# fp16 parts for the queries, keys and states of the last two attention blocks, and other orders in pairs 10 to 12

## What is computed

```python
x = x + attn(layernorm(x))
x = x + ffn(layernorm(x))

# attention, for each sequence and head; k is scaled to norm 1
attn    = (q @ k.T) * beta.T * decay                # within a chunk
y_local = attn @ v
delta   = v.T @ (k * beta * decay_to_end)
y       = (q @ state.T) * exp(cla) + y_local         # chunks in turn
state   = state * total_decay + delta

# ffn: Wg, Wu, Wd are 4-bit codes times scales
gate, up = xt @ Wg.T, xt @ Wu.T
out      = (gelu(gate) * up) @ Wd.T
```

## Time and profile before

| | us |
|---|---|
| median of 3 runs | 1116.49 (1115.62 to 1116.97) |
| the profiled execution | 1116.83 |
| its span, first to last instruction | 1115.1 |
| TensorE busy | 1107.1 |
| VectorE busy | 865.6 |
| GpSimd busy | 651.3 |
| ScalarE busy | 504.9 |

### The profile page before, as it was taken

One profiled execution on the slowest core, in us unless ns is written; L12 is line 12 of the kernel. 1 busy time (PEld: TensorE's weight loads), 2 busy tenths in 40 slices (PEclk: granted clock), 3 DMA queues, 4 the chain that ended last, 5 costly groups with the idle time before them and its releaser, 6 DMA issues.

```text
span 1115.1 us, 22523 instructions
## 1 busy us (share of the span) xinstructions
PE 1107.1 (99%) x8898; PEld 862.0 (77%) x8898; DVE 865.6 (78%) x1516; ACT 504.9 (45%) x1170; POOL 651.3 (58%) x665
## 2 busy tenths in 40 slices
PE   9999999999999999999999999999999999999999
PEld 5666656566457677788888888888888888888886
DVE  7788767468777766688988898889888888986664
ACT  4442345365244444444554454445444544454332
POOL 2376545236785656656775677567756775676330
PEclk9999999999999999999999999999999999999999
DMA  8021111000112323222323232323232323222222
GB/s 304 9 72 44 38 37 41 10 10 1 48 47 76 106 76 114 95 105 105 114 96 112 98 115 95 131 80 115 102 134 83 115 105 118 101 109 77 77 76 76
DMA packets 30233, 96.66 MB, mean 87 GB/s; under 512 B 3440, under 2 KB 3760, under 8 KB 23472
## 3 DMA queue, kind: packets, MB, share of 16 engines
q1 hardware_dynamic: 30128, 95.23, 24.3%
HBM read 63.73 MB, written 31.49 MB: 85 GB/s over the span
## 4 chain that ended last, share of the span: by engine, by line
PE 92%; DVE 3%; POOL 2%; ACT 1%; issue 1%; DMA 0%; SPq 0%; DVEq 0%; POOLq 0%; ACTq 0%
PE ps L649 44%; PE ps L718 19%; PE ps L466 9%; PE ps L758 7%; PE ps L610 6%; PE ps L432 1%; PE ps L552 1%; PE ps L541 1%; PE ps L562 1%; PE ps L476 1%; PE ps L532 1%; PE ps L554 0%; DMA WR<-wqkv 0%; DVE fw L1352 0%; ACT L938 0%
## 5 line engine op out<-in xcount | busy, mean ns | idle before, releaser
L649 PE MATMUL ps<-REG,WR 128*128 128x256 f16 x1344 | 183.3, 273 | 0.0
L649 PE MATMUL ps<-XT,WR 128*128 128x256 f16 x1344 | 183.3, 273 | 0.0
L1059 ACT COPY load<-ps 128x256 f32<-128x256 f32 x168 | 62.4, 371 | 228.8 <-PE ps L649 228.4
L649 PEld LDWEIGHTS ps<-REG,WR 128*128 128x128 f16 x1344 | 130.0, 98 | 21.0
L649 PEld LDWEIGHTS ps<-XT,WR 128*128 128x128 f16 x1344 | 131.5, 98 | 15.4
L1387 DVE SCALAR_TENSOR_TENSOR X<-ps,X 128x512 f32<-128x512 f32 x161 | 108.0, 683 | 16.2 <-PE ps L718 13.8
L1059 ACT COPY bigB<-ps 128x256 f32<-128x256 f32 x168 | 62.5, 372 | 127.6 <-PE ps L649 127.6
L1686 POOL TENSOR_TENSOR ihl_s<-fw,ihl_s 128x512 f16<-128x512 f32 (+1 forms) x46 | 49.5, 1088 | 116.7 <-ACT ihl_s L962 116.7
L1459 DVE TENSOR_TENSOR bigB<-bigB,ps 128x256 f32<-128x256 f32 x168 | 69.5, 414 | 60.2 <-ACT bigB L1059 38.6
L1459 DVE TENSOR_TENSOR load<-load,ps 128x256 f32<-128x256 f32 x168 | 68.7, 413 | 44.7 <-ACT load L1059 31.4
L649 PE MATMUL ps<-REG,bigA 128*128 128x256 f16 x672 | 91.7, 273 | 0.7 <-ACT bigB L1059 0.7
(11 more groups left out here) (244 smaller groups left out, 2536.8 us busy)
## 6 DMA issues: line engine op xcount, KB each, us to landing
kept<-X SPq DMA_DIRECT2D x26, 1024.0 KB, 3.9
X<-kept SPq DMA_DIRECT2D x26, 1024.0 KB, 5.7
load<-codes SPq DMA_DIRECT2D x48, 256.0 KB, 2.7
load<-scales SPq DMA_DIRECT2D x48, 256.0 KB
bigA<-cla SPq DMA_DIRECT2D x14, 256.0 KB, 3.2
X<-x SPq DMA_DIRECT2D x3, 1024.0 KB, 12.9
WR<-wqkv SPq DMA_DIRECT2D x2, 1024.0 KB, 9.5
y<-X SPq DMA_DIRECT2D x2, 1024.0 KB, 4.3
```

The costliest lines, as they stand in the source:

```text
L649: mm = eng.matmul(half_bank(kind, name), w(wp, kt), x(xp, kt), start=(first and n == 0), stop=(n == 5), skip_group_check=True)
L1059: eng.copy(start, half_bank(kind, name)).then_inc(s_snap, 1)
```

## The change

Queries, keys and states of the last two sequences (tiles 8 to 15) are kept as high and low fp16 parts in the place of the fp32 numbers. The scores and the product with the state become three fp16 matmuls for one fp32, and the transposes of k two matmuls with an fp16 identity. For this, in tiles 4 to 11, VectorE (k) and ScalarE (q) evict the full product in place in its bank, ScalarE casts the high part, and VectorE subtracts the low part, after which the bank is free. From tile 9 on ScalarE and VectorE make the parts of the state (`state_high`, `state_low`). The order on VectorE changes: the eviction of k goes ahead of the dequantization, and the low parts of keys, k, attention and q go ahead of the eviction of v. In the pairs, ScalarE's second `inter_high` goes behind the snapshot of P6 (pairs 9 to 16 and 63), VectorE's token sums in pairs 10 and 12 behind the sum `C12`, and GpSimd's low parts of chunk 13 behind `inter_low` of pair 11.

```diff
+RS = 2.0 ** 4
+SS = 2.0 ** -6
...
+        ident_h = bigD[:, 1152:1216].bitcast(F16)
...
+        qh, kh = ([REG[:, a, b, :].bitcast(F16).rearrange("p (s h t) -> p s h t", s=2, h=4) for b in range(2)]
+                  for a in range(2))
+        st_f, st_h = st[:, 0, :], two(st[:, 1, :].bitcast(F16))
...
+        def updated(T):
+            n = 3 * (T // 4) + T % 4 + 1
+            return (s_state, n) if T < SPLIT else (s_full["state"], n - 6)
...
+                cs = slice(128 * c, 128 * c + 128)
+                if T >= SPLIT:
+                    pe.wait_ge(s_setup, 8)
                 for h in range(4):
-                    t = eng.transpose(PS[kn][:, 128 * h:128 * h + 128],
-                                      kT[:, b % 2, h, 128 * c:128 * c + 128], ident[:, :])
+                    if T < SPLIT:
+                        t = eng.transpose(PS[kn][:, 128 * h:128 * h + 128], kT[:, b % 2, h, cs], ident[:, :])
+                    else:
+                        for p in range(2):
+                            t = eng.matmul(PS[kn][:, 128 * h:128 * h + 128], kh[b % 2][:, p, h, cs], ident_h[:, :],
+                                           start=(p == 0), stop=(p == 1))
                 t.then_inc(s_kn, 1)
...
                 for h in range(4):
-                    mm = eng.matmul(PS[4][:, 128 * h:128 * h + 128], kT[:, b % 2, h, 128 * c:128 * c + 128],
-                                    qT[:, b % 2, h, 128 * c:128 * c + 128], start=True, stop=True)
+                    scores = PS[4][:, 128 * h:128 * h + 128]
+                    if T < SPLIT:
+                        mm = eng.matmul(scores, kT[:, b % 2, h, cs], qT[:, b % 2, h, cs], start=True, stop=True)
+                    else:
+                        for kp, qp in ((0, 0), (0, 1), (1, 0)):
+                            mm = eng.matmul(scores, kh[b % 2][:, kp, h, cs], qh[b % 2][:, qp, h, cs],
+                                            start=(kp == qp == 0), stop=(kp == 1))
                 mm.then_inc(s_S, 1)
...
                     for h in range(4):
-                        mm = eng.matmul(PS[yg][:, 128 * h:128 * h + 128], qT[:, b % 2, h, 128 * c:128 * c + 128],
...
+                        else:
+                            for qp, sp_ in ((0, 0), (0, 1), (1, 0)):
+                                mm = eng.matmul(PS[yg][:, hs], qh[b % 2][:, qp, h, cs], st_h[:, sp_, hs],
+                                                start=(qp == sp_ == 0), stop=(qp == 1))
                     mm.then_inc(s_yg, 1)
 
                 if c < 3:
-                    dl = bank_of["dl", T] = banks.take(pe, (s_state, 3 * b + c + 1))
+                    dl = bank_of["dl", T] = banks.take(pe, updated(T))
...
                 if kind == "q":
                     ac.wait_ge(s_const, 64)
                     ac.wait_ge(s_mm["q"], 4 * b + h + 1)
+                    if b >= 2:
+                        bank = PS[bank_of["q", b, h]][:, :]
+                        ac.wait_ge(s_bqr, 1)
+                        eng.activation(bank, bank, ACT.Identity, bias=bqr[:, h:h + 1],
+                                       scale=RS / (XS * QS)).then_inc(s_full["q"], 1)
+                        ac.wait_ge(s_full["q"], 4 * b + h - 7)
+                        eng.copy(qh[b % 2][:, 0, h, :], bank).then_inc(s_part["q"], 1)
+                        return
...
+                elif kind == "k" and b >= 2:
+                    ac.wait_ge(s_full["k"], 4 * b + h - 7)
+                    eng.copy(kh[b % 2][:, 0, h, :], PS[bank_of["k", b, h]][:, :]).then_inc(s_part["k"], 1)
+
+            def state_high(T):
+                n = 3 * (T // 4) + T % 4
+                ac.wait_ge(s_full["state"], n - 5)
+                ac.wait_ge(s_yg, n)
+                eng.mul(st_h[:, 0, :], st_f, SS).then_inc(s_part["state"], 1)
...
                 norms_of_k(T)
                 if T + 1 < NT:
                     decay(T + 1)
+                if T > SPLIT and T % 4:
+                    state_high(T - 1)
+                if T >= SPLIT:
+                    keys_high(T)
                 for f in fill:
                     project(*f)
                 if T >= SPLIT:
-                    keys_high(T)
                     attention_high(T)
...
@@ -1130,8 +1181,9 @@
                     operands_high(m - 1)
                 elif m > 8:
                     inter_high(oo - 2)
+                snapshot("gate", m, "P6")
+                if m > 8 and m - 1 not in SEVEN_PAIRS:
                     inter_high(ee - 2)
-                snapshot("gate", m, "P6")
                 snapshot("gate", m, "P7")
...
                 elif kind == "k" and b >= 1:
                     dv.wait_ge(s_const, 64)
                     dv.wait_ge(s_mm["k"], done)
+                    if b >= 2:
+                        bank = PS[bank_of["k", b, h]][:, :]
+                        eng.tensor_scalar(bank, bank, f * RS, bqr[:, 4 + h:5 + h], ALU.mult,
+                                          ALU.add).then_inc(s_full["k"], 1)
+                        return
                     eng.tensor_scalar(kT[:, b % 2, h, :], PS[bank_of["k", b, h]][:, :], f, bqk_s[:, 4 + h:5 + h],
                                       ALU.mult, ALU.add).then_inc(s_qkv["k"], 1)
+
+            def project_low(kind, b, h):
+                if kind in "qk" and b >= 2:
+                    parts = (qh if kind == "q" else kh)[b % 2]
+                    dv.wait_ge(s_part[kind], 4 * b + h - 7)
+                    eng.tensor_tensor(parts[:, 1, h, :], PS[bank_of[kind, b, h]][:, :], parts[:, 0, h, :],
+                                      ALU.subtract).then_inc(s_qkv[kind], 1)
+
+            def state_low(T):
+                n = 3 * (T // 4) + T % 4
+                dv.wait_ge(s_part["state"], n - 5)
+                eng.scalar_tensor_tensor(st_h[:, 1, :], st_f, SS, st_h[:, 0, :], ALU.mult,
+                                         ALU.subtract).then_inc(s_state, 1)
...
+                        new = s_state if T < SPLIT else s_full["state"]
+                        eng.tensor_copy(st[:, s, :] if T < SPLIT else st_f, dl[:, :]).then_inc(new, 1)
...
+            eng.tensor_scalar(bqr[:, :], bqk_s[:, :], RS, None, ALU.mult).then_inc(s_bqr, 1)
...
             for T in range(NT):
                 i, fill = T - APART, fills(T)
+                split_k = [f for f in fill if f[0] == "k" and f[1] >= 2]
                 weigh_keys(T)
+                if T > SPLIT and T % 4:
+                    state_low(T - 1)
+                for f in split_k:
+                    project(*f)
                 if T == 0:
                     weigh(T)
                 if T == 1:
@@ -1511,13 +1590,18 @@
                     weigh(T)
                 if T >= 1:
                     apply("n2", T - 1)
+                if T >= SPLIT:
+                    keys_low(T)
+                for f in split_k:
+                    project_low(*f)
+                if T >= SPLIT:
+                    attention_low(T)
                 for f in fill:
-                    project(*f)
+                    if f not in split_k:
+                        project_low(*f)
+                        project(*f)
...
-                if T >= SPLIT:
-                    keys_low(T)
-                    attention_low(T)
                 if SPLIT <= T + 3 < NT:
                     value_low(T + 3)
...
                     token_sums(m // 2 - 2, 0, 2)
+                combine("gate", m, "C12")
                 if m in (10, 12):
                     token_sums(m // 2 - 3, 2, 4)
-                combine("gate", m, "C12")
...
+            eng.tensor_scalar(ident_h[:, :], ident[:, :], 1.0, None, ALU.mult).then_inc(s_setup, 1)
...
@@ -1826,6 +1912,8 @@
                 if m == 10:
                     token_sums(3)
                     token_low(2)
+                if m == 12:
+                    dequant(13)
                 if m == 13:
...
                         dq_difference(k)
                     dq_first_sums(k)
-                    dequant(k)
+                    if k != 13:
+                        dequant(k)
```

24 lines of the change are left out of this document (16 added, 8 removed).

## The result

The changed kernel took 1121.54 us (median of 5 runs, 1120.33 to 1121.80) beside 1116.58 of the kernel before in the same comparison: a ratio of 1.0043, 95% interval 1.0031 to 1.0054. It is slower by 5.0 us, where +2.5 was forecast. Its profiled execution took 1120.61 (span 1118.9); the one of before had a span of 1115.1.

The account below looks back on a forecast made before the run. TensorE was taken as the bound almost everywhere (busy 1107.1 of 1115.1 us). The sum 1.0 + 1.7 + 1.7 - 0.95 - 0.9 = +2.55 us gave 1119.0 against the median (1119.4 for the profiled execution); range 1112.0 to 1121.7.

Parts of the forecast that it names:

- Matmul time: TensorE, tiles 8 to 15: cheaper scores (1.78 us) and state products (1.57), transposes nothing; -3.35 us in all.
- Tile 6: Two subtractions ahead of v delay TensorE's start of kn in tile 6: +1.0 us, bounds 0.5 and 1.2.
- Tile 8 to 10: Queue ahead of v delays the GELU and inter; TensorE waits 2.65 us at k of tile 10: +1.7, bounds +0.8 and +2.3.
- Tile 12 to 15: VectorE, already late, gets low parts ahead of v, and state_low; TensorE starts tile 15 later: +1.7 us, bounds +0.8 and +2.5.
- Elsewhere: Tiles 10, 11 and 15, outside the delayed stretches: the matmul gain stays whole, -0.95 us.
- Pairs 10 to 12: Turned orders remove TensorE's waits for a snapshot and for GpSimd's low parts: -0.9 us, bounds -1.7 and +0.2.
- Set-up: The set-up instructions (bqr, ident_h) stand before stretches in which their engines idle: they cost nothing.
- The lock rival: state_low takes 1.45 us instead of 0.69 in tiles 9 and 13: 1120.5, or 1121.5 with slowed token sums; chance 0.10.
- half of it hides: Rival: chains of tiles 8 to 10 and 12 to 15 cost half, first stall 0.5: about 1116.5 us; chance 0.12.
- the parts hide: Rival: VectorE and ScalarE keep up and no new wait arises: 1112.2 us; chance 0.22.
- no wait was to stand in pair 12: Sign expected in the profile after: TensorE has no wait in pairs 11 and 12.

Follow-up runs that it names:

- a_v_first: The changed kernel with the eviction of v directly behind apply again, ahead of the low parts of keys, k, attention and q: 1115.45 us.
- a_v_middle: The changed kernel with the eviction of v ahead of the low parts of keys and attention, still behind those of k and q: 1116.51 us.
- b_two_orders: The kernel before with two pair orders, ScalarE's inter_high and GpSimd's low parts of chunk 13 moved, VectorE's token sums left in place: 1115.65 us.
- a_sums_back: The changed kernel with VectorE's two token sums of pairs 10 and 12 ahead of the sum C12 again: 1119.83 us.
- c_sums_late: The changed kernel with v behind apply, token sums ahead of C12, state_low behind keys_low, and the first block's four token sums later: 1112.31 us.

## Why the prediction was right or wrong, step by step

**Matmul time**, -3.35: right, to the term. The scores gave 0.22 each and the states 0.27 or 0.22, the transposes nothing.

**Tile 6**, +1.0 (0.5 to 1.2): +0.65, so near the lower bound, for the reason given there. The dequantization ahead of v took 1.29 us in its new place and 1.78 in the old one, and that 0.5 came off the 1.20 of the two subtractions.

**Tile 8 to 10**, +1.7 against before (0.8 to 2.3), a wait of 2.65: the wait is 2.66, and the difference went from +0.31 to +2.39, +2.1. The chain named is the one the timeline shows: v, cast, table load, GELU, `inter`, `turn_low`, TensorE. v was forecast at 185.1 and stood at 185.74, half of the difference because `inter` of tile 8 came 1.8 later (171.21 for 169.40) and not 1.5, half because `state_low` took 1.18 and not 0.69. The release came 0.6 later than forecast (191.72 for 191.1) and TensorE 0.5 later (188.28 + 0.67 = 188.95 for 188.44); that the wait came out to a hundredth is luck. a_v_first and a_v_middle show that the order is the cause.

**Tile 12 to 15**, +1.7 (0.8 to 2.5): from +1.68 at tile 12 to +4.20 at `kn` of tile 15, +2.5, at the edge of the bounds. The mechanism was right, its size wrong: the term for `state_low`, 0 and 0.6, was mis-sized. It took 1.09 and 1.05. In tile 13 it took the place of a wait for GpSimd of 0.58 and still cost 0.3: from `weigh_keys` to `apply` VectorE needs 2.45 (249.25, 251.70), 2.13 before (246.37, 248.50). In tile 14 it stood whole ahead of `apply` and cost 1.0 (2.18 for 1.20). That is 0.7 of the 0.8 that was missing. TensorE also met the waits at `apply` in the main (1.99, 1.04), and at the `gather` only with 0.61.

**Elsewhere**, -0.95: -1.2. The difference went from +2.39 at k of tile 10 to +1.68 at `kn` of tile 12, -0.7 where -0.5 was said, and from +4.20 at `kn` of tile 15 to +3.72 at pair 8 (322.93, 326.65). The gain is whole, as forecast; two states and one score of tiles 10 and 11 are more than 0.50, and the rest of them was counted with tiles 12 to 15.

**Pairs 10 to 12**, -0.9: +0.1, and this step failed. For two of the orders its number holds (b_two_orders, -1.0), though not its terms. Of VectorE's sums behind C12 it said that the snapshot behind them is no earlier, and left it at that; but they are later. ScalarE's casts wait for them, and snapshots stand behind the casts. In pair 10 this cost 0.4 at a combine that now came too late, and 0.3 at the snapshot (0.63 for 0.37 in a_sums_back). Of pair 12 the step said nothing, and there a wait of 0.94 came. Half of it (0.49 in a_sums_back, 0.52 in b_two_orders) is there without VectorE's order: the sums take 2.7 us, 1.41 in before, beside GpSimd's work that was made later. The other half is VectorE's order. I had counted a moved instruction only where it went away from, not for those who wait for it, or run beside it, in its new place.

**Set-up**, 0: it brought -0.66, at tile 1.

**The lock rival** was true in kind and smaller in size: `state_low` took 1.05 to 1.18 us in five of its six tiles and 0.68 in one, so 0.4 to 0.5 more and not 0.76. The 0.76 came from L1451, which has other instructions of GpSimd beside it; what `state_low` pays is what is left of GpSimd's instruction (below); in tiles 9, 13 and 14 that lies on the chain which TensorE waits for.

**The clock** is in no step. Where a prediction says that TensorE will wait 2.65 us at once, the clock belongs in the range. On the footing of the profiled executions 1119.4 was forecast and 1120.6 came, 1.2 more; the median lies 2.5 above its forecast, about 1 of it from the clock.

**The number.** The direction and the chain were right, and each of the waits forecast in the tiles is there. But 1121.54 lies only 0.2 inside the upper bound of 1121.7, and luck has a part in that: the pairs (+1.0) and tiles 8 to 15 (+1.2) came out dearer than forecast, and the set-up (-0.66), tile 6 (-0.35) and the rest of the tiles (-0.25) cheaper. It is also the 1121.5 of the lock rival, but not by its terms. By its own terms the rival that half of it hides makes 1116.7 to 1117.5 and not 1116.5. That the parts hide is refuted by the wait of 2.66, and that half of it hides by +2.1 and +2.5 in the two chains. Of the signs named, one failed: no wait was to stand in pair 12, and one of 0.94 does.

## What to carry to other kernels

Before an instruction is put ahead of another in an engine's queue, follow what waits for the one that is pushed back, through all engines to the bound one, and compare the sum of what is put ahead with the smallest margin on that way; here 0.6 us each ahead of v was free in some tiles and full price in others, and the same instructions with v first made a kernel 6.1 us faster (1115.45 and 1121.54, of two comparisons; about 1 of it is the clock). A saving on the engine that bounds the kernel counts only where the others keep pace: from tile 13 to 15 TensorE followed VectorE, and shorter matmuls became longer waits until VectorE's own chain was cut (c_sums_late). Split a change of several orders and price each: two of the three in the pairs gained 1.0, the third gave 1.2 back.

## What the runs showed of the hardware

**A wait can cost more than its length.** With an idle time of 2.66 us a lowered mean granted clock (0.998 or 0.997) was recorded in 10 of 19 executions (changed kernel and a_sums_back), with 1.10 and 2.66 close together in 6 of 6, and in none of the 88 of the nine kernels whose longest wait, behind the first 2 us, was 1.25. The two of these executions that were profiled show the fall to 0.50 in the wait of 2.66, and none at the waits of 1.98 and 1.04. The Trainium skill, "TensorE: Matmul & The Clock Gate", section "HAM oscillation — how this bites in real kernels", reckons with a fall only for gaps longer than this one; here the measurement decides.

**VectorE with two SBUF operands waits for GpSimd to end.** `state_low` (L1287) of tiles 10, 13, 14 and 15 in the changed kernel, and the GpSimd instruction under way when each starts:

```profile
196.15 1.18 DVE L1287 SCALAR_TENSOR_TENSOR bigA<-bigA 128x512 f16<-128x512 f32 x1
...
249.88 1.09 DVE L1287 SCALAR_TENSOR_TENSOR bigA<-bigA 128x512 f16<-128x512 f32 x1
...
263.22 1.05 DVE L1287 SCALAR_TENSOR_TENSOR bigA<-bigA 128x512 f16<-128x512 f32 x1
...
275.02 0.68 DVE L1287 SCALAR_TENSOR_TENSOR bigA<-bigA 128x512 f16<-128x512 f32 x1
...
195.75 1.04 POOL L1756 TENSOR_TENSOR bigB<-bigB,kn_s 128x512 f32<-128x512 f32 x1
...
249.38 1.04 POOL L1756 TENSOR_TENSOR bigB<-bigB,kn_s 128x512 f32<-128x512 f32 x1
...
263.09 0.64 POOL L1738 TENSOR_SCALAR_AFFINE_SELECT bigB<-bigB 128x512 f32<-128x512 f32 x1
...
274.51 1.02 POOL L1711 TENSOR_TENSOR rs<-rs,half 128x1 f32<-128x1 f32 x1
```

Add start and length: GpSimd's end at 196.79, 250.42 and 263.73, VectorE's at 197.33, 250.97 and 264.27, always 0.54 or 0.55 later (in tiles 9 and 11 too), whatever the overlap. Alone it takes 0.68. So by these five it gets the operands when GpSimd is done, and its price is what is left of GpSimd's instruction, less 0.14. The Trainium skill, "SBUF — State Buffer", section "SBUF: two separate sides", states this as an exclusive lock for the whole instruction, and these rows agree. The last pair is no clear exception: `state_low` took 0.68 there although the power on 128x1 (L1711) was under way until 275.53. But this power takes 0.57 in tile 13 (251.10) and 1.02 here, where it began during VectorE's token sums (L1524, two SBUF operands, 273.71 to 275.10), so here it may have been GpSimd that waited for VectorE. No run tries that.
